# Cross-attention with normalised residual: six context loads over six turns, all head products first in the prologue, and gamma, beta and bo by repeating loads

## What is computed

```python
q = (x   @ Wq + bq).reshape(16, 100, 16, 64)
k = (ctx @ Wk + bk).reshape(16, 1444, 16, 64)
v = (ctx @ Wv + bv).reshape(16, 1444, 16, 64)
attn = softmax(einsum('bqhd,bkhd->bhqk', q, k) / 8)
out  = einsum('bhqk,bkhd->bqhd', attn, v).reshape(16, 100, 1024) @ Wo + bo
z = x + out
y = (z - mean(z)) * rsqrt(var(z) + 1e-5) * gamma + beta
```

## Time and profile before

| | us |
|---|---|
| median of 3 runs | 870.71 |
| lowest, highest | 869.03, 873.26 |
| the profiled execution, its own time | 871.59 |
| its span | 869.8 |
| PE busy in the span | 846.3 |
| ACT busy, DVE busy, POOL busy | 779.6, 774.7, 569.1 |

### The profile page before, as it was taken

One profiled execution on the slowest core, in us unless ns is written; L12 is line 12 of the kernel. 1 busy time (PEld: TensorE's weight loads), 2 busy tenths in 40 slices (PEclk: granted clock), 3 DMA queues, 4 the chain that ended last, 5 costly groups with the idle time before them and its releaser, 6 DMA issues.

```text
span 869.8 us, 19632 instructions
## 1 busy us (share of the span) xinstructions
PE 846.3 (97%) x7306; PEld 605.2 (70%) x7306; DVE 774.7 (89%) x938; ACT 779.6 (90%) x1132; POOL 569.1 (65%) x575
## 2 busy tenths in 40 slices
PE   7999999999999999999999999999999999999996
PEld 6676776767677766777667776776767777677675
DVE  4988888999989989999899998999899999999984
ACT  5899999989999989999989999998989989999983
POOL 2283997949566693867749586694956669397301
PEclk9999999999999999999999999999999999999999
DMA  7899999999999999999999999999999999999985
GB/s 198 186 211 192 195 210 189 216 200 223 215 209 217 217 204 224 209 226 211 205 213 221 216 208 229 198 227 217 213 215 220 205 233 208 222 188 217 209 183 117
DMA packets 683939, 180.80 MB, mean 208 GB/s; under 512 B 654596, under 2 KB 683076, under 8 KB 683844
## 3 DMA queue, kind: packets, MB, share of 16 engines
q1 hardware_dynamic: 682372, 179.01, 105.7%
q10 hardware_dynamic: 1344, 0.53, 0.3%
q0 software_dynamic: 128, 0.01, 0.0%
HBM read 15.35 MB, written 0.82 MB: 19 GB/s over the span
## 4 chain that ended last, share of the span: by engine, by line
PE 52%; ACT 14%; DVE 13%; DMA 8%; issue 7%; SPq 4%; ACTq 0%; POOLq 0%; POOL 0%; DVEq 0%
PE ps L670 25%; PE ps L631 22%; DMA pt_hi<-p_hi 7%; DVE p_lo L932 6%; ACT p L1072 6%; ACT p_hi L1080 5%; DVE nmax L917 4%; SPq L429 2%; PE ps L495 2%; PE ps L488 2%; SPq L420 1%; ACT unused L1023 1%; DMA bq_pairs<-in_L_xattn_bq_dram 1%; DVE rsum L923 1%; ACT o_t L1110 1%
## 5 line engine op out<-in xcount | busy, mean ns | idle before, releaser
L932 DVE SCALAR_TENSOR_TENSOR p_lo<-p,rinv,p_hi 128x1444 f16<-128x1444 f32 x200 | 370.9, 1855 | 7.5 <-ACT p_hi L1080 7.0
L917 DVE TENSOR_REDUCE nmax<-ps 128x1 f32<-128x1446 f32 x200 | 330.0, 1650 | 18.8 <-PE ps L631 18.3
L1080 ACT ACTIVATE p_hi<-p,rinv 128x1444 f16<-128x1444 f32 x200 | 300.0, 1500 | 32.1 <-DVE rinv L925 28.5
L1072 ACT ACTIVATE p<-ps,nmax 128x1446 f32<-128x1446 f32 x200 | 292.2, 1461 | 17.8 <-DVE nmax L917 15.4
L670 PE MATMUL ps<-pt_hi,c_hi 128*128 128x256 f16 (+1 forms) x1232 | 252.9, 261 | 11.4 <-DMA pt_hi<-p_hi 9.0
L670 PE MATMUL ps<-pt_hi,c_lo 128*128 128x256 f16 (+1 forms) x1232 | 253.0, 261 | 0.0
L631 PE MATMUL ps<-ct_hi,g_hi 128*128 128x482 f16 (+3 forms) x624 | 155.5, 367 | 0.8 <-DVE g_lo L892 0.7
L631 PE MATMUL ps<-ct_lo,g_hi 128*128 128x482 f16 (+3 forms) x624 | 154.9, 366 | 0.0
L631 PE MATMUL ps<-ct_hi,g_lo 128*128 128x482 f16 (+3 forms) x624 | 154.9, 366 | 0.0
L670 PEld LDWEIGHTS ps<-pt_hi,c_hi 128*128 128x128 f16 x1232 | 114.1, 98 | 50.4 <-issue 16.8
L1204 POOL TENSOR_TENSOR g_raw<-g_raw,gb_b 128x400 f32<-128x400 f32 x60 | 81.0, 1350 | 96.2 <-ACT g_raw L1096 96.2
(11 more groups left out here) (138 smaller groups left out, 863.0 us busy)
## 6 DMA issues: line engine op xcount, KB each, us to landing
c_raw<-in_ctx_dram SPq DMA_DIRECT2D x32, 256.0 KB, 6.1
pt_hi<-p_hi SPq DMA_TRANSPOSE x200, 3.5
pt_lo<-p_lo SPq DMA_TRANSPOSE x200, 3.7
c_raw<-in_ctx_dram SPq DMA_DIRECT2D x16, 192.0 KB
c_raw<-in_ctx_dram SPq DMA_DIRECT2D x48, 18.0 KB
out_dram<-late_sb SPq DMA_DIRECT2D x16, 50.0 KB
x_sb<-in_x_dram SPq DMA_DIRECT2D x1, 600.0 KB
o_t<-in_L_xattn_Wq_dram SPq DMA_DIRECT2D x2, 256.0 KB, 4.5
```

The lines of the kernel that those rows point to most:

```text
L917: dve.tensor_reduce(nmax[:, n % RING:n % RING + 1], ps[:, bank:bank + 3, 0:KEYW], AX.XY, ALU.max, negate=True).then_inc(s_nm, 1)
L932: dve.scalar_tensor_tensor(out=p_lo[:, n % LOS, 0:KL], in0=p32[:, n % P32S, 0:KL], scalar=rinv[:, i:i + 1], in1=p_hi[:, par, 0:KL], op0=AL ...
L1072: act.activation(p32[:, n % P32S, :].rearrange("p (k w) -> p k w", w=KEYW), ps[:, bank:bank + 3, 0:KEYW], ACT.Exp, bias=nmax[:, i:i + 1], ...
L1080: act.activation(p_hi[:, par, 0:KL], p32[:, n % P32S, 0:KL], ACT.Copy, scale=rinv[:, i:i + 1]).then_inc(s_hi, 1)
```

## The change

Three things change.

- A context is loaded in six pieces of two tiles (`load_tiles`), at r = 0 to 5; the last piece has one whole tile and the three copies of the tail. The wait for POOL's copy stands at r = 0. Each half of a context has a semaphore of its own, and each half of ACT's sum waits for its own. The store stands at r = 10. Context 1, in the prologue, comes in six pieces too; context 0 is loaded as before.
- In the prologue all head products come first; J_X follows them. ACT empties J_B as well, DVE empties J_X and makes `gb_sb`.
- gamma and beta are loaded into all 128 partitions of `rows_b`, and bo into `bo_b`, by DMAs that read the row 128 times. PE's three spreading matmuls go, and DVE adds 128x128 numbers of `bo_b` where it copied 128x384.

```diff
--- before.py
+++ after.py
@@ -47,7 +47,8 @@
     PTS = 3
     FIRST_TILES = 9
     LOS = 3
-    LOADS = 6
+    TL = 2
+    NL = KT // TL
     TG = 4
     NT = KT // TG
     HG = 4
@@ -61,8 +62,8 @@
 
     G_AT = 1
     G_AT_FIRST = 4
-    LOAD_AT = 1
-    STORE_AT = 2
+    LOAD_AT = 0
+    STORE_AT = 10
     CHI_AT = (4, 6, 7)
     FIN_AT = 6
     SUM_AT = (5, 8)
@@ -172,8 +173,7 @@
         ax_un = sb("ax_un", [P, 2])
         ax_scale = sb("ax_scale", [P, 2])
         g_un = sb("g_un", [P, 1])
-        rows_sb = sb("rows_sb", [1, 3, P])
-        ones_row = sb("ones_row", [1, P])
+        bo_b = sb("bo_b", [P, P])
         table = sb("table", [P, 1])
         x_sb = sb("x_sb", [QL, B, D])
         xT = sb("xT", [P, B, QL])
@@ -225,13 +225,12 @@
         s_wo = sem("wo_loaded")
         s_x = [sem(f"x_loaded{i}") for i in range(2)]
         s_cf = [sem(f"first_context_loaded{g}") for g in range(NT)]
-        s_c = [sem(f"context_loaded{i}") for i in range(2)]
+        s_c = [[sem(f"context_loaded{i}_{half}") for half in range(SUMS)] for i in range(2)]
         s_bq = sem("bq_loaded")
         s_bvl = sem("bv_loaded")
         s_top = sem("context_max_spread")
         s_axt = sem("ax_max_spread")
         s_part_id = sem("identity_over_range_ready")
-        s_const = sem("constants_set")
         s_id0 = sem("identity_zeroed")
         s_ident = sem("identity_ready")
         s_zero = sem("key_padding_zeroed")
@@ -308,15 +307,15 @@
         s_y = sem("y_ready")
         s_out = [sem(f"stored{i}") for i in range(2)]
 
-        J_A, J_X, J_B = 4, 6, 7
-        J_G = J_B + 2
+        J_A, J_B, J_X = 4, 6, 8
+        J_G = J_X + 1
         J_V0, J_V1, J_M0, J_M1, J_M2, J_M3, J_X1, J_X2, J_X3, J_R = range(J_G + NG, J_G + NG + 10)
         N_PRO = J_R + 1
         J_M = (J_M0, J_M1, J_M2, J_M3)
         A_JOBS = (J_A, J_A + 1, J_B, J_B + 1)
         BANKS = {J_X: 0, J_B: O_BANK, J_B + 1: JOB_BANK, J_G: 1, J_G + 1: 2, J_G + 2: 3, J_G + 3: 4,
                  J_V0: O_BANK, J_V1: O_BANK, J_M2: O_BANK, J_M3: O_BANK}
-        BY_SCALAR = [1, 3, J_A, J_A + 1, J_X, J_B + 1, J_V1, J_M2]
+        BY_SCALAR = [1, 3, J_A, J_A + 1, J_B, J_B + 1, J_V1, J_M2]
         BY_VECTOR = [k for k in range(N_PRO) if k not in BY_SCALAR]
         ONCE = {0: (J_V0,), 1: (J_V1, J_M0), 2: (J_M1, J_M2), 3: (J_M3,), 8: (J_X1,), 9: (J_X2,), 10: (J_X3,), 17: (J_R,)}
         FIRST_TOP = 3
@@ -352,8 +351,8 @@
             first = g // 2 * 2 * HG + g % 2
             return slice(first, first + 2 * HG - 1, 2)
 
-        def context_landed(b):
-            return 16 * LOADS * (b // 2 + b % 2)
+        def context_landed(b, half):
+            return 16 * (NL // SUMS + (3 if half == SUMS - 1 else 0)) * (b // 2 + b % 2)
 
         def emptied(eng, k):
             if k in BY_VECTOR:
@@ -369,28 +368,31 @@
 
         @block.sync
         def _(sp):
-            def load_context(b, g):
-                a, e = TG * g, min(TG * g + TG, KT - 1)
-                par, landed = b % 2, s_c[b % 2] if b else s_cf[g]
-                whole = ctx_in[b:b + 1, a * P:e * P, :].rearrange("o (t p) d -> p (o t) d", p=P)
-                sp.dma_start(c_raw[:, par, a:e, :], whole).then_inc(landed, 16)
-                if g == NT - 1:
+            def load_tiles(b, a, e, landed):
+
+                par, whole = b % 2, min(e, KT - 1)
+                sp.dma_start(c_raw[:, par, a:whole, :],
+                             ctx_in[b:b + 1, a * P:whole * P, :].rearrange("o (t p) d -> p (o t) d", p=P)).then_inc(landed, 16)
+                if e == KT:
                     tail = ctx_in[b:b + 1, (KT - 1) * P:KL, :].rearrange("o p d -> p o d")
                     for i in range(3):
                         sp.dma_start(c_raw[i * KTAIL:(i + 1) * KTAIL, par, KT - 1:KT, :], tail).then_inc(landed, 16)
+
+            def load_context(b, i):
+                load_tiles(b, TL * i, TL * (i + 1), s_c[b % 2][i * SUMS // NL])
 
             for half in range(2):
                 cols = slice(half * D_H // 2, (half + 1) * D_H // 2)
                 sp.dma_start(w_raw[0][:, cols], Wq[:, cols]).then_inc(s_w[0][half], 16)
             sp.wait_ge(s_zero, 1)
             for g in range(NT):
-                load_context(0, g)
+                load_tiles(0, TG * g, TG * (g + 1), s_cf[g])
             sp.dma_start(x_sb[:, 0:XG, :], x[0:XG, :, :].rearrange("b q d -> q b d")).then_inc(s_x[0], 16)
             for half in range(2):
                 cols = slice(half * D_H // 2, (half + 1) * D_H // 2)
                 sp.dma_start(w_raw[2][:, cols], Wv[:, cols]).then_inc(s_w[2][half], 16)
-            for g in range(NT):
-                load_context(1, g)
+            for i in range(NL):
+                load_context(1, i)
 
             def transpose_context_hi(b):
                 par = b % 2
@@ -443,7 +445,7 @@
                     break
                 transpose_hi(n)
                 w, r = window(n)
-                if LOAD_AT <= r < LOAD_AT + NT and w + 2 < B:
+                if LOAD_AT <= r < LOAD_AT + NL and w + 2 < B:
                     if r == LOAD_AT:
                         sp.wait_ge(s_chl, w + 1)
                     load_context(w + 2, r - LOAD_AT)
@@ -569,10 +571,10 @@
             for k in range(4):
                 emptied(pe, k)
             head_products_by_two(w_t[0], w_t[1], 0, J_A)
+            head_products_by_two(w_t[0], w_t[1], 2, J_B)
             query_bias(take(J_X))
             spread_context_max(job_bank(J_G + 2), 0)
             transpose_x(0, J_X).then_inc(s_fill, 1)
-            head_products_by_two(w_t[0], w_t[1], 2, J_B)
             for k in (J_A, J_A + 1, J_X):
                 emptied(pe, k)
             for g in range(NG):
@@ -584,15 +586,10 @@
 
             def bias_rows(k):
                 bank = take(k)
-                pe.wait_ge(s_small, 16 * 3)
-                pe.wait_ge(s_const, 1)
                 pe.wait_ge(s_bvw, 1)
                 for c in range(PAIRS):
-                    pe.matmul(bank[:, 0:P], bv_wide[:, c, :], wo_sb[:, c, :], start=(c == 0), stop=False)
-                pe.matmul(bank[:, 0:P], ones_row[:, :], rows_sb[:, 0, :], start=False, stop=True)
-                pe.matmul(bank[:, P:2 * P], ones_row[:, :], rows_sb[:, 1, :], start=True, stop=True)
-                pe.matmul(bank[:, 2 * P:3 * P], ones_row[:, :], rows_sb[:, 2, :], start=True,
-                          stop=True).then_inc(s_fill, 1)
+                    mm = pe.matmul(bank[:, 0:P], bv_wide[:, c, :], wo_sb[:, c, :], start=(c == 0), stop=(c == PAIRS - 1))
+                mm.then_inc(s_fill, 1)
 
             def once(k):
                 if k in (J_V0, J_V1):
@@ -793,7 +790,8 @@
                 half = 0 if k == J_V0 else 4
                 last = copy(w_t[2][:, half:half + 4, :], split(bank, 4, P))
             elif k == J_R:
-                last = copy(rows_b[:, :, :], split(bank, 3, P))
+                eng.wait_ge(s_small, 16 * 3)
+                last = eng.tensor_tensor(rows_b[:, 0, :], bank[:, 0:P], bo_b[:, :], ALU.add)
             elif k in J_M:
                 last = scaled(m_sb[:, every_other(J_M.index(k)), :], split(bank, HG, P), 1.0 / P_RANGE)
             else:
@@ -832,11 +830,10 @@
             dve.memset(c_max[:, NT:NT + 1], C_LEAST).then_inc(s_cleast, 1)
             dve.memset(p_lo[:, :, KL + 2 * KTAIL:KT * P], 0.0)
             dve.memset(ax_parts[:, :, :], 0.0).then_inc(s_axz, 1)
-            dve.memset(ones_row[:, :], 1.0).then_inc(s_const, 1)
 
             def context_max(g):
 
-                dve.wait_ge(s_cf[g], 16 if g < NT - 1 else 16 * (LOADS - NT + 1))
+                dve.wait_ge(s_cf[g], 16 if g < NT - 1 else 16 * 4)
                 dve.tensor_reduce(c_max[:, g:g + 1], c_raw[:, 0, TG * g:TG * g + TG, :].rearrange("p t d -> p (t d)"),
                                   AX.X, ALU.max, apply_absolute_value=True).then_inc(s_am, 1)
                 if g == NT - 1:
@@ -874,7 +871,8 @@
             for g in range(NT):
                 context_max(g)
             context_scale(0, job_bank(J_G + 2))
-            empty(J_B)
+            empty(J_X)
+            dve.tensor_scalar(gb_sb[:, :], job_bank(J_X)[:, XG * QL:XG * QL + H], SCALE, None, ALU.mult).then_inc(s_gb, 1)
             for g in range(NT):
                 tiles = slice(TG * g, TG * g + TG)
                 dve.wait_ge(s_chi, g + 1)
@@ -1023,8 +1021,8 @@
                 act.activation(unused[0:rows, 0:data.shape[1]], data, ACT.Abs, accum_out=total).then_inc(s_sum, 1)
 
             def context_sum(b, i):
+                act.wait_ge(s_c[b % 2][i], context_landed(b, i))
                 if i == 0:
-                    act.wait_ge(s_c[b % 2], context_landed(b))
                     act.wait_ge(s_cm, b)
                 tiles = slice(KT // SUMS * i, KT // SUMS * (i + 1))
                 magnitudes(summed("context", b, i), P, c_raw[:, b % 2, tiles, :].rearrange("p t d -> p (t d)"),
@@ -1037,14 +1035,11 @@
```

(9 more changed lines are left out.)

## The result

The changed kernel takes 875.1 us (median of 20 runs, 871.0 to 879.5), the kernel before, on the same chip, 870.9 (20 runs, 868.2 to 875.1). The ratio is **1.0038**, 95% interval 1.0023 to 1.0054. That is slower, by less than the 0.5% that the prediction called measurable, though the interval excludes no change. The forecast was 865.0 with a range up to 872.0: wrong in sign and outside the range.

A forecast was written before the change was run, and what follows sets the result against it. PE, busy 97% of the span, was taken as the bound. Loads -4.7, turn 17 -0.9 and prologue -0.1 summed to -5.7 us: 865.9 for the profiled execution, 865.0 as forecast, range 860.5 to 872.

The forecast's parts named there:

- The five waits in turns 7 and 8 go: Steady part: PE's five waits for high-part transposes, 4.95 us shown and 5.7 us in all, taken as gone.
- I add 1.0 us: Steady part: 1.0 us allowed for new lateness at pair ends and windows with less spare; nothing to 5 us possible.
- (b): SP's queue, turns 5 to 10: the burst moves and delays the context's transposes; slower, 875.8 us; chance 0.12.
- About 2 us of shorter landing in the worst case: Transpose of r = 4: landing after issue falls from 5.48 us to the usual 3.5.
- 25 us of SP's time in all, beside PE's work: SP's queue: three more issues of about 0.59 us in each of 14 windows, beside PE's work.
- Turn 17, -0.9 us: Turn 17: PE's three spreading matmuls, 98.95 to 99.82, go; PE is the bound, so 0.9 us is gained.
- The prologue, -0.1 us, with +0.64 from 0.192 MB at 300 GB/s: Prologue: up to -0.7 us from reordering against +0.64 for the repeating loads; -0.1 taken, ends -0.7 and +1.3.
- They run at 2.4 GHz in about half of their 2.0 us; they fit: Prologue: the second set of head products moves into PE's idle 1.33 us before bq, at full clock.
- The store at r = 10 and SP's wait one turn earlier at nothing: SP's queue: moving the store from r = 2 and the wait for POOL's copy one turn earlier costs nothing.
- (c): Steady part: the pieces do not change when transposes land; only turn 17 and prologue act, 869.7 us; chance 0.13.
- (a): Steady part: the waits go, but half of their time was already made up; 868.4 us; chance 0.15.
- the 84 us: DMA queue: 2.0 us fixed for each of 3 x 14 added DMAs, slower if exclusive; the sum used issue times instead.

The follow-up runs named there:

- b1: Kernel before, its loads cut into six pieces, two in each of turns 1 to 3, tail at r = 3 and store at r = 2 as before: 1.0055, 876.1 us.
- d1: Kernel before, with an unused 2 KB DMA on SP behind each of its three loads per window: 1.0089, 879.0 us.
- b4: Kernel before, with the tails of contexts 2 to 15 issued by POOL at the start of a window instead of by SP: 0.9949, 866.9 us.
- b2: Kernel before, with its three loads at r = 0, 1 and 2 and the store at r = 10: 0.9956, 867.9 us.
- c3: Kernel before, with three loads from r = 0, store at r = 10, tails by POOL, and repeating row loads issued after the prologue: 0.9926, 865.3 us.
- a1: Kernel before, with only the load change: six pieces at r = 0 to 5, their semaphores, store at r = 10: 1.0053, 875.6 us.
- a3: Kernel before, with only gamma, beta and bo by repeating loads and without the three spreading matmuls: 1.0030, 872.7 us.
- c1: Kernel before, with only the rows by repeating loads, issued by POOL after the prologue at about 25 us: 0.9982, 869.8 us.
- a2: Kernel before, with only the prologue's order changed, all head products first, and the copies moved between ACT and DVE: 1.0002.
- d3: As c3, with all head products first in the prologue as well: 0.9940 to the kernel before, 866.3 us.
- c4: The changed kernel, with its three repeating loads issued by POOL after the prologue: 0.9995 to the kernel before, 871.1 us.
- b3: As a1, but with the three tails issued with the first piece at r = 0 instead of at r = 5: 0.9983 to the kernel before, 869.8 us.
- a4: The changed kernel without the repeating loads, bo, gamma and beta as before: 1.0024 to the kernel before, 872.9 us.

## Why the prediction was wrong, step by step

- **"The five waits in turns 7 and 8 go."** They went. The reading of the earlier trace rows was right: the burst of turn 3 makes them. b1 and d1, which add issues to it, raise PE's waits to 12.8 and 13.6 us; b4, which takes the tails out of it, and b2, which starts it a turn earlier, lower them to 3.9 and 2.9.
- **"I add 1.0 us" for new waits: the step that failed.** Its ground was a turn's account: 3.6 us of issues in 4.2, 5.0 in turn 5, "the queue has caught up before the context's own transposes of turns 7 and 8". Summed over SP's timeline from 27 us on, the kernel before already spends 726 us in issues and 45 us in the short gaps between them, of 843 us: 3.9 us of a 4.2 us turn on average. A transpose of `p_hi` or `p_lo` takes 1.56 us in the mean, not 1.44, since some take 2 to 3.5 us, and not in the burst alone: 46 of 432 transposes take over 2 us before, 32 after and 48 in c3. The row that said so, 3.09 us in context 5, was read as a sign of the burst and moved to rival (b). After the change the queue is 0.6 us behind at r = 7 (1.0 in a1, 0.25 before) and falls further behind with the context's transposes, to 2.1 us at r = 9. PE's waits, forecast to go from 9.0 - 4.95 + 1.0 to about 5 us, are 9.6 (11.9 in a1): with the other eight waits taken as staying, the new ones cost 5.6 (7.9) where 1.0 was put. In time, loads only is +4.6 us (0.53% of 870.9) where -4.7 was forecast, off by 9 us.
- **ACT's waits.** They rose from 3.6 to 9.1 us (12.9 in a1), and the prediction asked about PE only. They are a sign of the late queue and were not seen to make it later. Where ACT had so waited before it wrote a high part, SP never began that part's transpose as soon as ACT ended, in none of the seventeen kernels; after the change it came to it 0.75 to 2.95 us later. A way through the low part, which needs the high one, isn't excluded.
- **"About 2 us of shorter landing in the worst case."** It didn't come: with pieces of half the size, as many transposes land over 5 us after their issue began as before (13 against 15).
- **"25 us of SP's time in all, beside PE's work."** d1 tests this sentence by itself: three tiny issues per window, 21 us of SP's time, cost 0.89%, 7.8 us of 870.9. SP's queue is on the path, though the page's busy times don't list SP. (How much of it is the added packets is open, as said above.)
- **Turn 17, -0.9 us.** Right: from the start of the bias products to the next scores it is 2.75 us before (97.07 to 99.82) and 1.79 after (101.72 to 103.51), 0.96 less. The steady parts of a3 and c1 are 2.1 and 2.4 us shorter than before, which includes it; the surplus may be the scatter of single executions.
- **The prologue, -0.1 us, with +0.64 from 0.192 MB at 300 GB/s.** The mechanism was right and the size wrong by a factor of three to four: the context's maximum is 2.0 us late in a3 (13.05 against 11.06) and 2.7 in the changed kernel, the first scores' maximum 2.5 and 4.6, with the clock's part in them. Bytes at the rate of the earlier trace rows are not the price of a load that reads one row 128 times. Even the end of the range, +1.3, was too small; the half rate that it took for small packets is in no row.
- **"They run at 2.4 GHz in about half of their 2.0 us; they fit."** They did, with no gain in a2. There the clock was at half for 6.8 us and in the changed kernel for 10.2 instead of 3.4, but d1 has 10.2 us too with the old order, so that the order isn't shown to be the reason. In d3, where it was 3.4 again, the first maximum did come 1.5 us earlier than in c3 (20.7 against 22.2), but the ratios of the two overlap.
- **The store at r = 10 and SP's wait one turn earlier at nothing.** Nothing speaks against it: b2 contains both and is faster. Neither was tried alone.
- **Rivals.** (b) was right in place and sign, and its 875.8 is near the measured 875.1, in part by luck: it had no cost for the prologue, where the rows' loads turned out to take about 0.4% (1.0038 against 0.9995 in c4), and 0.9 us of new waits in 13 windows, more than the trace shows. Its chance, 0.12, was too low for a queue that rows showed full. (c) was right in its condition, since the time from issue to landing stayed as it was, and wrong in what it drew from it: a1 and b3 differ by 0.70% through the place of the tails alone. (a) would have needed the waits to go, and in the change they don't; in b2, where they fall by 6.1 us in a trace 3.6 us below its median, the ratio gives 3.8 us back, so that a part being made up elsewhere isn't excluded.

The Trainium skill, "DMA: Bandwidth & Descriptors", section "Measured (HBM→SBUF, 128 partitions, SWDGE, issued from GpSimd)", advises against cutting transfers. The direction holds here: b1 is 0.55% slower than three loads in the same turns. Its fit of 2.0 us fixed per DMA stands in the section "🔬 Anatomy of one DMA — SWDGE (gpsimd) path" and is for DMAs that POOL issues, while SP issues these. The landings here look as if they had a fixed part of that kind: 2 KB land in 2.8 us in the median (d1), 128 KB in 2.6 (a1), 256 KB in 3.4 (b4). But it overlaps other work: the 84 us that the prediction worked out from it didn't appear, and a transpose lands as long after its issue as before. What the runs price is the issues on SP's queue.

**What stays open.** Why single transposes take 2 to 3.5 us to issue was not tried apart; a full queue fits (they come while loads and other transposes are under way, and the DMA engines are busy all through the steady part), no run isolates it. Whether part of b4's gain is POOL's earlier start and not its own queue is open too. Why a4 is better than a1, and the whole better than its parts, isn't settled: the length of the half-clock stretch in the prologue differs from execution to execution (first maxima from 20.7 to 26.7 us over these kernels), and the intervals allow chance. What held bq back in the changed kernel, and why b2's shift by one turn takes so many of PE's waits away, aren't settled. The steady gain of 2 us in a3 and c1, more than turn 17's, is open as well.

## What to carry to other kernels

Make an account for each engine that issues DMAs, as for a computing engine: issues per turn by their measured mean and not their median, the gaps between them included, and take out whatever need not be there (another engine's queue gained 0.5%, a start one turn earlier 0.4%) before cutting transfers into more pieces. Don't put short issues right in front of a group of transposes that has to be on time. Here, loads that repeat a row belonged behind the prologue, where no first load waits behind them. And a prologue is judged by many executions, not by the first maximum of one.
